# First product of the second routed layer in three rounded products, with the operands split on VectorE two slots ahead

## What is computed

```python
scores = jnp.einsum('bsh,he->bse', x, wr) + br
expert_id = jnp.argmax(scores, axis=-1)
h = jnp.einsum('bsh,ehf->ebsf', x, w1) + b1[:, None, None, :]     # 128 -> 512
h = jax.nn.gelu(h, approximate=False)
y = jnp.einsum('ebsf,efh->ebsh', h, w2) + b2[:, None, None, :]    # 512 -> 128
one_hot = jax.nn.one_hot(expert_id, E, dtype=x.dtype)
out = jnp.einsum('ebsh,bse->bsh', y, one_hot)
```

## Time and profile before

| | |
|---|---|
| median of 3 runs | 1395.06 us (1391.64 to 1395.79) |
| the profiled execution | 1390.68 us |
| its span, first to last instruction | 1388.5 us |
| mean granted TensorE clock | 0.934 of full speed |
| TensorE busy over the span | 88% (matmuls), 69% (weight loads) |
| VectorE, ScalarE, GpSimd busy | 72%, 59%, 56% |
| the second routed layer | from about 1224 us to the end |

### The profile page before, as it was taken

How to read it: one execution, slowest core, us unless ns; L and a number is a source line. 1 busy time by engine, 2 the same in 40 slices (tenths; PEclk the granted TensorE clock), 3 DMA queues, 4 the chain that set the end, 5 groups by cost and what they waited for, 6 DMA issues and landing times. The chain is left out here.

```text
span 1388.5 us, 32705 instructions
## 1 busy us (share of the span) xinstructions
PE 1222.3 (88%) x9994; PEld 957.1 (69%) x9994; DVE 997.8 (72%) x3311; ACT 826.0 (59%) x1707; POOL 778.1 (56%) x943
## 2 busy tenths in 40 slices
PE   3899999999987999999999991887399999659998
PEld 1566767666655777777777771776277777559997
DVE  4698998999746789999999995676378888612222
ACT  2354554545327888888888870555177777535554
POOL 3467777778641235545455454333658887526666
PEclk8999999999867999999999995999599999879999
DMA  2333122222312231121211313776311222288771
GB/s 98 94 101 96 59 78 77 70 71 64 87 42 81 45 69 41 51 62 44 64 44 46 83 28 77 194 197 182 107 28 63 67 62 58 70 315 281 260 262 60
DMA packets 82985, 134.54 MB, mean 97 GB/s; under 512 B 14834, under 2 KB 42747, under 8 KB 82896
## 3 DMA queue, kind: packets, MB, share of 16 engines
q1 hardware_dynamic: 60896, 96.94, 24.4%
q0 software_dynamic: 9856, 21.52, 5.0%
q10 hardware_dynamic: 12144, 15.00, 3.8%
HBM read 95.60 MB, written 30.47 MB: 91 GB/s over the span
## 5 line engine op out<-in xcount | busy, mean ns | idle before, releaser
L1280 DVE TENSOR_TENSOR m_Sl<-m_S,m_Sh 128x512 fp32r<-128x512 f32 x256 | 206.2, 816 | 38.7 <-ACT m_S L1202 37.1
L1197 ACT ACTIVATE m_Sh<-PS,W 128x512 fp32r<-128x512 f32 x256 | 177.4, 693 | 60.1 <-PE PS L1120 43.0
L1202 ACT ACTIVATE m_S<-PS,W 128x512 f32<-128x512 f32 x256 | 176.1, 688 | 7.9 <-DVE m_Sl L1280 7.9
L1581 POOL DMA_INDIRECT rows<-r_row,r_posi x128 | 136.2, 1064 | 34.5 <-issue 33.1
L850 DVE TENSOR_TENSOR am<-PS,C 128x512 f32<-128x512 f32 x192 | 119.6, 679 | 24.1 <-PE PS L478 23.6
L1118 PE MATMUL PS<-m_HH,m_w1h 128*128 128x512 f32 x256 | 107.3, 419 | 17.5 <-ACT m_S L1202 11.1
L1824 PEld LDWEIGHTS PS<-f_wt,f_hid 128*128 128x128 f32 x960 | 119.6, 192 | 4.1
L1813 PE MATMUL PS<-f_xT,f_wt 128*128 128x256 f32 x480 | 120.1, 387 | 0.0
L1824 PE MATMUL PS<-f_wt,f_hid 128*128 128x128 f32 x960 | 120.0, 275 | 0.0
L1135 PE MATMUL PS<-m_Sl,m_w2h 128*128 128x512 f32 x256 | 102.8, 402 | 1.4 <-DVE m_Sl L1280 0.7
L1132 PE MATMUL PS<-m_Sh,m_w2h 128*128 128x512 f32 x256 | 102.0, 398 | 1.3 <-DVE m_oe L1266 1.3
(11 more groups left out here) (251 smaller groups left out, 3074.2 us busy)
## 6 DMA issues: line engine op xcount, KB each, us to landing
f_wt<-wr SPq DMA_DIRECT2D x40, 578.0 KB, 4.1
f_row<-rows SPq DMA_DIRECT2D x40, 260.0 KB, 2.9
f_wt<-wr SPq DMA_DIRECT2D x40, 256.0 KB, 2.8
m_gb<-gates SPq DMA_DIRECT2D x8, 1024.0 KB, 7.9
m_raw<-gates SPq DMA_DIRECT2D x8, 1024.0 KB, 8.0
sb<-z_rows ACTq DMA_DIRECT2D x15, 512.0 KB, 5.3
f_row<-rows SPq DMA_DIRECT2D x40, 132.0 KB, 2.1
mid<-f_res SPq DMA_DIRECT2D x20, 256.0 KB, 3.3
```

What stands on the lines that cost most here:

```text
L1197: nc.scalar.activation(Sh[:, n % 4, :], PS[:, n % 3, :], ACT.Silu, bias=w("b1")[:, n:n + 1]).then_inc(sh_ready, 1)
L1202: nc.scalar.activation(S[:, n % 3, :], PS[:, n % 3, :], ACT.Silu, bias=w("b1")[:, n:n + 1]).then_inc(s_ready, 1)
L1280: nc.vector.tensor_tensor(Sl[:, n % 4, :], S[:, n % 3, :], Sh[:, n % 4, :].bitcast(F32), ALU.subtract).then_inc(sl_ready, 1)
L1581: nc.gpsimd.indirect_dma_start(out=self.rows, out_offset=bass.IndirectOffsetOnAxis(ap=self.posi[:, u, t:t + 1], axis=0), in_=self.row[:, u ...
```

## The change

Layer 1 alone is changed. `up` no longer reads the fp32 operands. It makes each of its four chunks from three fp32r matmuls of the same shape (128x128 weights, 256 columns), and it waits for two new semaphores, `x_split` and `w_split`, in place of `xT_ready`. ScalarE's copy of the transposed rows writes the rounded high part `xh` in place of `xT`. VectorE gets three more instructions for each slot: the low part of x (`xl` = PSUM - `xh`), the rounded high part of the first weight matrix (`w1h`, a copy of 128x512) and its low part (`w1l`, a subtraction of 128x512, behind a wait for that copy). It does these for slot s + 2 at the head of its step s, before the instructions that were there; slots 0 and 1 are split ahead of the loop. The second product and layer 0 stay as they were.

```diff
+        if layer:
+            xh = sb("xh", [P, 2, SLOT], F32R)
+            xl = sb("xl", [P, 2, SLOT], F32R)
+            w1h = sb("w1h", [P, 2, chunks * P], F32R)
+            w1l = sb("w1l", [P, 2, chunks * P], F32R)
...
             def up(s, u, turn):
                 pe.wait_ge(weights_in[u], 16 * (turn + 1))
+                if layer:
+                    pe.wait_ge(x_split, s + 1)
+                    pe.wait_ge(w_split, s + 1)
+                    v = u % 2
+                    for f in range(chunks):
+                        bank, half = divmod(f, 2)
+                        to = PS[:, 2 + 2 * v + bank, half * SLOT:(half + 1) * SLOT]
+                        cols = slice(f * P, (f + 1) * P)
+                        nc.tensor.matmul(to, w1h[:, v, cols], xh[:, v, :], start=True, stop=False)
+                        nc.tensor.matmul(to, w1h[:, v, cols], xl[:, v, :], start=False, stop=False)
+                        mm = nc.tensor.matmul(to, w1l[:, v, cols], xh[:, v, :], start=False, stop=True)
+                    mm.then_inc(h_psum, 1)
+                    return
...
-                nc.scalar.activation(xT[:, v, :], PS[:, v, 0:SLOT], ACT.Copy).then_inc(xT_ready, 1)
+                nc.scalar.activation(xh[:, v, :] if layer else xT[:, v, :], PS[:, v, 0:SLOT], ACT.Copy).then_inc(xT_ready, 1)
...
+            def split_x(s, v):
+
+                if since(s, 2):
+                    dve.wait_ge(h_psum, s - 1)
+                dve.wait_ge(xT_ready, s + 1)
+                nc.vector.tensor_tensor(xl[:, v, :], PS[:, v, 0:SLOT], xh[:, v, :].bitcast(F32), ALU.subtract).then_inc(x_split, 1)
+
+            def split_weights(s, u, turn):
+
+                v = u % 2
+                dve.wait_ge(weights_in[u], 16 * (turn + 1))
+                if since(s, 2):
+                    dve.wait_ge(h_psum, s - 1)
+                w1 = wt[:, u, 0:chunks * P]
+                nc.vector.tensor_copy(w1h[:, v, :], w1).then_inc(w_high, 1)
+                dve.wait_ge(w_high, s + 1)
+                nc.vector.tensor_tensor(w1l[:, v, :], w1, w1h[:, v, :].bitcast(F32), ALU.subtract).then_inc(w_split, 1)
...
             def step(s, u, turn):
                 if layer:
+                    if not isinstance(s, int) or s + 2 < NSLOT:
+                        split_x(s + 2, u % 2)
+                        split_weights(s + 2, (u + 2) % DEPTH, turn + (u + 2) // DEPTH)
                     take_token(s, u, turn)
                     add_x(s, u, turn)
                     return
...
-            if not layer:
+            if layer:
+                for s in range(2):
+                    split_weights(s, s, 0)
+                    split_x(s, s)
+            else:
                 find_tokens(dve)
```

More of the change, by code:

```diff
@@ L1719, in routed @@
         xb_ready = sem("xb_ready"); centred_ready = sem("centred_ready")
+        w_high = sem("w_high"); w_split = sem("w_split"); x_split = sem("x_split")
         found = sem("found"); res_ready = sem("res_ready"); told_done = sem("told_done")
```

## The result

| | before | after |
|---|---|---|
| median | 1394.05 us (6 runs, 1391.64 to 1395.79) | 1384.1 us (6 runs, 1377.01 to 1384.95) |
| ratio | | 0.9917, 95% interval 0.9893 to 0.9942 |
| profiled execution | 1390.68 us | 1379.1 us |
| its span | 1388.5 us | 1376.9 us |
| start of `res` to start of `res`, steady state | 3.73 us | 3.43 us |

What follows compares the result with a forecast made beforehand. The prediction took TensorE's issue of matmuls as the bound. 39 slots x 0.24 = 9.4 us plus 0.4 for slot 0 and the start make 9.8; 1395.06 - 9.8 = 1385.2 us, range 1377 to 1398.

Steps and rivals of the forecast that it cites:

- The place: Layer 1's steady state: TensorE's issue of matmuls sets the end, at 3.74 us per slot, with nothing else late.
- The price of a record: TensorE's `up` in layer 1: an fp32r record of 256 columns costs 124 ns, saving 0.24 us per slot.
- my two readings of the row: Price of a 256-column fp32r record: 115 ns in proportion to the 512-column record, 124 ns with 17 ns fixed.
- The split: VectorE's added work per slot, 1.0 to 2.5 us, is hidden under 3.50 us of TensorE.
- the bare price: Layer 1's split without its cover: 1.52 us would stand bare in each slot, 40 times that is 61 us.
- The start: Start of layer 1: `up` 0.1 us late, slot 0's `up` gains about 0.8, taken as +0.4 us of gain.
- GpSimd: `told` and two indirect DMAs per slot, slowed beside VectorE to 3.37 us, stay under 3.50 and cost nothing.
- The milder rival: POOL or DVE ends layer 1's slot at 3.6 to 3.8 us: -6 to +2 us, 1389 to 1397; chance 0.15.
- The two terms: Layer 1's gains: 9.4 us from 39 slots of 0.24, and 0.4 us for slot 0 and the start.

## Why the prediction was right

**The place.** TensorE's issue set the slot, and still does; `res` waits for the second product in both. Held.

**The price of a record.** I took 124 ns from a range of 107 to 230, with the 17 ns of the 512-column record as a fixed cost. Measured: 119 ns. 12 ns on 107 at 256 columns and 17 on 213 at 512: part of it is fixed and part grows with the columns, and the truth lies between my two readings of the row. The term was mis-sized: 0.24 us per slot was forecast, 0.30 came (8 x 0.216 - 12 x 0.119 = 0.30), 11.4 us over the slots for 9.4. By the rule max(60, 6 + columns) cycles of the Trainium skill ("VectorE: DVE Perf Modes", on the errata of SBUF-source ops) it would by estimate have been 109 ns, 0.42 us per slot; the trace does not agree for fp32r.

**The split.** VectorE was to be through 0.8 us before `res` was due: 0.91. `w_split` was to come 1.3 us early: `w1l` ends at 1292.41 and its `up` starts at 1293.60, 1.2. The kernel with the split alone took the time of before, so "hidden" is measured, not argued. What I said of the bare price was wrong: 61 us if the cover were gone, at 1.52 us per slot. The kernel with the split one slot ahead lost about twice that: 2.1 us per slot, since the split then also waits behind `res`, and 47 us by the clock, which my sum had at nothing.

**The start.** 0.1 late was forecast, and from the weights' arrival it was 0.1, but for another reason than mine: my sum let the split fill the 1.54 us between the weights and `up` without asking what filled them before. It was the wait for the rows of slot 1, and it covered the split. The layer's head gained 0.9 and not 0.4. The first product gave 0.7 of the 0.8 that I expected; the rest of the difference is that I had set aside up to 2 us for VectorE's claim on the weights of slots 1 and 2, which cost nothing to be seen.

**GpSimd.** Here I was right in the verdict and wrong in the sum. I charged 0.23 us of contention to each of three instructions, 3.37 us in all. In the trace of after, `told` and both DMAs take 1293.85 - 1290.81 = 3.04, against 2.99 before. The 0.32 us by which these 2.99 exceed the 2.67 of the tail I had put down to VectorE, `told` above all; they are not contention, since the first DMA starts 0.71 us after `told` whenever `told` had waited for `res`, and 0.39 us after it in the tail. The mixture's contention was not a price per instruction but one of phase: it falls on a GpSimd instruction that starts inside a VectorE instruction with two SBUF inputs, or inside the copy, and only as far as that one still runs. In the mixture itself the 1.50 us were those of a DMA that started 0.01 us behind a subtraction; the one of 0.96 started when a subtraction had 0.03 us left. The milder rival's 3.78 us, which adds every block in full, was a ceiling that the phases never reached; the longest slot of GpSimd's in the kernels with one product was 3.54 us on the even chips (3.74 on the uneven one). Of the rule that I quoted from the Trainium skill ("SBUF — State Buffer", on who interferes with whom), the trace agrees that a copy, or a subtraction with two SBUF inputs, that started first holds up GpSimd. It does not agree that whoever issues first blocks the other in both directions: 37 subtractions of the changed kernel started inside a GpSimd instruction and took their ordinary 0.69 us.

**The time.** 1385.2 us was forecast and 1384.1 measured. Part of that nearness is luck: the profiled span fell by 11.6 us and the ratio gives 11.6 (0.0083 x 1394), both more than the 9.8 of my sum, while the medians differ by 9.95. The two terms were too small by 2.0 and 0.5 us, and the 0.6 us by which the layer started later took some of it back.

## What to carry to other kernels

Where TensorE issues without a gap, count its records and columns: an fp32 matmul of 256 columns cost 432 ns here, and three fp32r ones 357, so that a split into three products pays by 17% of that product even though it is three times the instructions. The operands' split is free only as long as it is made before TensorE wants it, so ask where in the other engine's order it falls: two slots ahead it cost nothing, one slot ahead some 128 us. Room on an engine is best measured by putting work there until the time moves, and a contention that was seen in one phase isn't a price for another.

## What the runs showed of the hardware that I had not expected

- With 1.85 us of idle time ahead of each first product, TensorE's granted clock fell to 1.2 GHz within 30 of 38 slots and held in the other eight; it was 0.77 on average from 1290 to 1320 us.
- An indirect DMA on GpSimd, 0.98 to 1.00 us otherwise, ended 0.85 to 0.89 us after a VectorE subtraction of two SBUF operands, or a copy from SBUF to SBUF, that had started before it and still had over 0.12 us to run (321 of 343 times in this layer, all runs together; in the other 22 the two had started within 0.05 us of each other, the DMA took its ordinary time and the VectorE instruction some 0.05 us more): 1.46 us with 0.59 left in the kernel with two more subtractions (1301.55), 1.39 with 0.52, 1.16 with 0.30. With 0.12 left or less it took its ordinary 0.98, 22 times in the kernel with one more subtraction.
- From the start of `told` to the start of the first indirect DMA it is 0.71 us, whether `told` lasts 0.37 us beside `xb` (1303.07 to 1303.78 in the earlier trace rows) or 0.19 (1290.81 to 1291.52). The longer `told` had cost nothing. Where GpSimd hadn't waited before it and `told` took its 0.23 us, the same stretch is 0.39 to 0.40 us.
- Between two chips the same kernel took 1390 and 1430 us, and the gain of the change was 0.8% on one and 0.4% on the other; 39.6 of the 42.5 us between the two profiles of the changed kernel lay ahead of the changed layer.
